# Four of 32 embedding fields fetched by one-hot products on TensorE instead of by gathers, in a DLRM tower on one Trainium2 core

## The chip, the cores and the metric

One Trainium2 chip, one NeuronCore of it. The metric is the device time of one execution in microseconds (us), the median over the runs. Engines: TensorE (PE in the rows; PEld is its weight load), VectorE (DVE), ScalarE (ACT), GpSimd (POOL) and SyncE (SP, which here only issues DMAs).

## What is computed

```python
e = stack([tbl_f[ids[:, f]] for f in range(32)], axis=1)     # 2048 samples x 32 fields x 256
dots = einsum('bnd,bmd->bnm', e, e)                          # 32 x 32 per sample
z = dots[:, iu, ju]                                          # the 496 pairs i < j
h = concatenate([z, dense_ctx], axis=1)                      # 496 + 16
h = maximum(h @ W_top1 + b_top1, 0)                          # 512 x 512
h = maximum(h @ W_top2 + b_top2, 0)                          # 512 x 256
y = h @ W_top3                                               # 256 x 1
```

All is float32. The tables have 1000, 1250 or 12500 rows of 256 numbers; the smallest, of 1000 rows, are nine.

## The kernel before

The work is 2048 samples of 32 fields, that is 65,536 table rows of 1 KB. One indirect DMA of GpSimd (a gather, L121) brings 128 rows: 4 samples ("a quad") with their 32 fields, field by field on 32 partitions. There are 512 gathers. Two of them are a unit; there are 256 units, and 16 row buffers of one unit each (ROWS), so GpSimd may be 16 units ahead of TensorE: before gather pair u it waits for the transposes of unit u-16 (L118).

For each unit TensorE makes four 128x128 transposes (L134, function transposes), ScalarE copies the result from PSUM to SBUF (evacuate, L207), and one unit later TensorE makes 32 small products (gram, L147): for each of 8 samples and two halves of the 256 columns, the 32x32 matrix of dot products. Eight units (16 quads, 64 samples) fill a PSUM bank; then VectorE spreads it with 16 copies (regroup, L240) into `pairs`, where 128 samples are one tile. There are 16 tiles. For a tile TensorE makes layer 1 (64 products, L160), ScalarE its ReLU (relu1, L216), TensorE layer 2 (16 products, L172), VectorE its ReLU (relu2, L251), TensorE layer 3 (L179), VectorE takes the score (L257), and SP stores it.

Each engine works through its list in order, and that list is written by hand: TensorE goes through transposes(u), gram(u-1), and puts layer 1 of the tile before behind the third unit of a tile, layer 2 behind the tenth and layer 3 behind the thirteenth. SP loads the indices first and then the dense features and the weights; w1 is 2 MB in 128 rows of 16 KB.

Of the kernel before, what the change touches and what calls it, by code (L numbers as in the profile page):

```python
# [5 lines left out]
F32 = mybir.dt.float32  # L6
U32 = mybir.dt.uint32
# [3 lines left out]
P = 128  # L11
N_FIELDS = 32
QUAD = P // N_FIELDS


def dlrm_tower(nc, index_t, base_t, dense_t, table, w1_t, b1_t, w2, b2_t, w3_t, out):
# [3 lines left out]
    NQ = index_t.shape[1]  # L20
# [4 lines left out]
    UQ, FQ, TQ = 2, 16, P // QUAD  # L25
    UNITS, TILES = NQ // UQ, NQ // TQ
    UPF, FPT = FQ // UQ, TQ // FQ
    UPT = UPF * FPT
    M1C, M2C = H1 // P, H2 // P
    KC = N_FIELDS // QUAD  # L30
    ROWS, COLS = 16, 6
    EARLY = 16
    assert HALVES == 2 and ND <= N_FIELDS and UNITS % ROWS == 0

    with ExitStack() as ctx:  # L35
# [8 lines left out]

        raw = sb("raw", [P, NQ], U32)
        base = sb("base", [P, 1], U32)
        index = sb("index", [P, NQ], U32)
        rows = [sb(f"rows{r}", [P, UQ, D]) for r in range(ROWS)]
        cols = [sb(f"cols{r}", [P, HALVES, UQ, P]) for r in range(COLS)]
# [3 lines left out]
        score = sb("score", [1, TILES, P])  # L53
# [5 lines left out]
        identity = sb("identity", [P, P])  # L59

        ps_turn = [pb(f"ps_turn{k}", [P, HALVES, UQ, P]) for k in range(2)]
        ps_gram = [pb(f"ps_gram{k}", [P, FQ, N_FIELDS]) for k in range(2)]
        ps_l1 = pb("ps_l1", [P, M1C, P])
        ps_l23 = pb("ps_l23", [P, 512])

# [7 lines left out]
        identity_zeroed, identity_ready = sem("identity_zeroed"), sem("identity_ready")  # L73
        w1_loaded, w_loaded = sem("w1_loaded"), sem("w_loaded")
        l1_done, hidden1_ready = sem("l1_done"), sem("hidden1_ready")
        l2_done, hidden2_ready = sem("l2_done"), sem("hidden2_ready")
        l3_done, score_ready = sem("l3_done"), sem("score_ready")
        stored = sem("stored")
# [3 lines left out]
        @block.sync  # L82
        def _(sp):
            sp.dma_start(base[:, :], base_t).then_inc(index_loaded[0], 16)  # L84
            sp.dma_start(raw[:, 0:EARLY], index_t[:, 0:EARLY]).then_inc(index_loaded[0], 16)
            sp.dma_start(raw[:, EARLY:NQ], index_t[:, EARLY:NQ]).then_inc(index_loaded[1], 16)
# [6 lines left out]
            load_dense(1)  # L93
            sp.dma_start(b1_sb[:, :], b1_t).then_inc(w_loaded, 16)
            sp.dma_start(b2_sb[:, :], b2_t).then_inc(w_loaded, 16)
            sp.dma_start(w3_sb[:, :], w3_t).then_inc(w_loaded, 16)
            sp.dma_start(w1_sb[:, :, :], w1_t).then_inc(w1_loaded, 16)
            sp.dma_start(w2_sb[:, :, :], w2.rearrange("(m p) n -> p m n", p=P)).then_inc(w_loaded, 16)
            for n in range(TILES):
                if n + 2 < TILES:  # L100
                    sp.wait_ge(l1_done, n + 1)
                    load_dense(n + 2)
                sp.wait_ge(score_ready, n + 1)
                sp.dma_start(out[n:n + 1, :], score[:, n, :]).then_inc(stored, 16)
            sp.wait_ge(stored, 16 * TILES)

        @block.gpsimd
        def _(pool):
            pool.memset(identity[:, :], 0.0).then_inc(identity_zeroed, 1)  # L109
            pool.wait_ge(identity_zeroed, 1)  # L110
# [3 lines left out]
            for u in range(UNITS):  # L114
                if UQ * u == EARLY:
                    pool.wait_ge(index_ready, 2)
                if u >= ROWS:
                    pool.wait_ge(transposed, u - ROWS + 1)  # L118
                for k in range(UQ):
                    q = UQ * u + k  # L120
                    pool.indirect_dma_start(  # L121
                        out=rows[u % ROWS][:, k, :], out_offset=None, in_=table,
                        in_offset=bass.IndirectOffsetOnAxis(ap=index[:, q:q + 1], axis=0),
                    ).then_inc(gathered[u % ROWS], 16)

        @block.tensor
        def _(pe):
            def transposes(u):
                pe.wait_ge(gathered[u % ROWS], 16 * UQ * (u // ROWS + 1))
                if u >= 2:  # L130
                    pe.wait_ge(cols_ready, u - 1)
                for h in range(HALVES):
                    for k in range(UQ):
                        last = pe.transpose(ps_turn[u % 2][:, h, k, :],  # L134
                                            rows[u % ROWS][:, k, h * P:(h + 1) * P], identity[:, :])
                last.then_inc(transposed, 1)

            def gram(u):
                f = u // UPF
                pe.wait_ge(cols_ready, u + 1)  # L140
                if u % UPF == 0 and f >= 2:
                    pe.wait_ge(pairs_ready, f - 1)
                for k in range(UQ):
                    for h in range(HALVES):
                        for j in range(QUAD):
                            x = cols[u % COLS][:, h, k, N_FIELDS * j:N_FIELDS * (j + 1)]
                            last = pe.matmul(ps_gram[f % 2][N_FIELDS * j:N_FIELDS * (j + 1), UQ * (u % UPF) + k, :],  # L147
                                             x, x, start=(h == 0), stop=(h == HALVES - 1))
                last.then_inc(gram_done, 1)

            def layer1(n):
                pe.wait_ge(pairs_ready, FPT * (n + 1))
# [31 lines left out]
            for u in range(UNITS):  # L184
                transposes(u)
                if u >= 1:
                    gram(u - 1)
                n, at = u // UPT - 1, u % UPT
                if n >= 0:
                    if at == 2:  # L190
                        layer1(n)
                    if at == UPF + 1:
                        layer2(n)
                    if at == UPF + 4:
                        layer3(n)
            gram(UNITS - 1)
# [5 lines left out]
        def _(act):  # L202
            def evacuate(u):
                act.wait_ge(transposed, u + 1)
                if u >= COLS:
                    act.wait_ge(gram_done, u - COLS + 1)
                act.copy(cols[u % COLS][:, :, :, :], ps_turn[u % 2][:, :, :, :]).then_inc(cols_ready, 1)  # L207
# [11 lines left out]
            for u in range(UNITS):  # L219
                evacuate(u)  # L220
                n, at = u // UPT - 1, u % UPT
                if n >= 0 and at == 3:
                    relu1(n)
# [3 lines left out]
        def _(dve):  # L227
            def make_index(i, q0, q1):
                dve.tensor_tensor(index[:, q0:q1], raw[:, q0:q1], base[:, 0:1].broadcast_to([P, q1 - q0]), ALU.add  # L229
                                  ).then_inc(index_ready, 1)  # L230

            def regroup(f):
                n, u = f // FPT, f % FPT
                dve.wait_ge(gram_done, UPF * (f + 1))
# [20 lines left out]
            def take_score(n):  # L255
                dve.wait_ge(l3_done, n + 1)
                dve.tensor_copy(score[:, n, :], ps_l23[0:1, H2:H2 + P]).then_inc(score_ready, 1)  # L257
# [4 lines left out]
            make_index(0, 0, EARLY)  # L262
            dve.wait_ge(index_loaded[1], 16)
            make_index(1, EARLY, NQ)
            for f in range(UNITS // UPF):
                regroup(f)
                n, at = f // FPT - 1, f % FPT
                if n >= 0 and at == 0:
                    relu2(n)
                    take_score(n)  # L270
# [45 lines left out]
```

## Time and profile before

| What | Value |
|---|---|
| median of 3 runs | 672.66 us (671.53 to 675.78) |
| the profiled execution, whole | 671.6 us |
| its span, first to last instruction | 669.8 us |
| mean granted TensorE clock | 0.781 of full speed |
| TensorE matmul busy | 502.9 us, 75% |
| GpSimd busy | 484.8 us, 72% |
| VectorE, ScalarE busy | 203.6 us (30%), 164.8 us (25%) |

Between the span and the whole execution lie 1.8 us. A busy share says how long an engine had an instruction in work, not whether anything waited for it; the views below say that.

### The profile page before, as it was taken

To read this page: it belongs to the slowest core of one execution; us is meant where nothing else is said; L and a number is where in the kernel's file an instruction comes from. 1 tells how busy PE (TensorE), PEld (TensorE's weight loads), DVE (VectorE), ACT (ScalarE), POOL (GpSimd) and SP (SyncE) were. 2 spreads that over 40 slices of the span, in tenths; PEclk is the share of its full clock that TensorE was granted. 3 is DMA by queue.
4 is the path that set the end of the run, shared out by engine and by line. 5 is a ranking of instruction groups with operands and counts; after the bars stand their busy time and mean duration, and the time that the engine had idled before them with its cause. 6 is when DMAs were issued, how large, how long until landed. Compare 5 with 4: busy or idle time off the path is not lost.

```text
span 669.8 us, 23188 instructions
## 1 busy us (share of the span) xinstructions
PE 502.9 (75%) x10560; PEld 416.9 (62%) x10560; DVE 203.6 (30%) x564; ACT 164.8 (25%) x321; POOL 484.8 (72%) x518
## 2 busy tenths in 40 slices
PE   2668778696886968778696877959679696877847
PEld 1547567485764847567485755848567484755736
DVE  0213433204343132433304343231433313343330
ACT  1222213222142222313222141222313222141310
POOL 6777777777777777777777777777777777777730
PEclk9857859687696877859688695977959597696958
DMA  7333333333333333333333333333333333333310
GB/s 246 109 104 111 107 107 109 106 109 106 106 110 104 111 106 107 109 104 112 105 107 110 104 112 104 108 109 103 111 106 109 108 104 109 106 108 109 105 57 0
DMA packets 26753, 71.65 MB, mean 107 GB/s; under 512 B 9232, under 2 KB 10144, under 8 KB 26528
## 3 DMA queue, kind: packets, MB, share of 16 engines
q0 software_dynamic: 24576, 67.14, 34.4%
q1 hardware_dynamic: 2080, 3.03, 1.3%
q8 instruction: 83, 1.36, 0.8%
q14 instruction: 14, 0.11, 0.1%
HBM read 70.13 MB, written 0.01 MB: 105 GB/s over the span
## 4 chain that ended last, share of the span: by engine, by line
POOL 38%; PE 25%; issue 15%; DMA 11%; DVE 9%; ACT 2%; SPq 0%; ACTq 0%
POOL rows L121 38%; PE ps_l L160 15%; DMA rows<-in_table,index 11%; DVE pairs L240 9%; PE ps_turn L134 6%; PE ps_gram L147 3%; ACT hidden L216 1%; PE ps_l L172 1%; ACT cols L207 1%; DMA raw<-in_index_t 0%; DVE hidden L251 0%; PE ps_l L179 0%; SPq L84 0%; DVE score L257 0%; ACTq L35 0%
## 5 line engine op out<-in xcount | busy, mean ns | idle before, releaser
L121 POOL DMA_INDIRECT rows<-in_table,index x512 | 484.1, 946 | 157.6 <-issue 142.2
L240 DVE COPY pairs<-ps_gram 32x128 f32<-32x128 f32 (+1 forms) x512 | 188.2, 368 | 422.9 <-PE ps_gram L147 416.4
L134 PE MATMUL ps_turn<-identity,rows 128*128 128x128 f32 x1024 | 207.1, 336 | 135.2 <-DMA rows<-in_table,index 134.6
L207 ACT COPY cols<-ps_turn 128x512 f32<-128x512 f32 x256 | 148.8, 590 | 482.5 <-PE ps_turn L134 482.5
L134 PEld LDWEIGHTS ps_turn<-identity,rows 128*128 128x128 f32 x1024 | 135.0, 167 | 158.1 <-DMA rows<-in_table,index 139.8
L160 PE MATMUL ps_l<-pairs,w_sb 128*128 128x128 f32 x1024 | 149.3, 319 | 22.6 <-DVE pairs L240 22.6
L160 PEld LDWEIGHTS ps_l<-pairs,w_sb 128*128 128x128 f32 x1024 | 146.2, 233 | 24.6 <-DVE pairs L240 24.5
L147 PEld LDWEIGHTS ps_gram<-cols 128*32 128x32 f32 x8192 | 104.8, 126 | 62.7 <-issue 55.3
L147 PE MATMUL ps_gram<-cols 128*32 128x32 f32 x8192 | 135.5, 214 | 4.3 <-ACT cols L207 3.6
L172 PE MATMUL ps_l<-hidden,w_sb 128*128 128x128 f32 x256 | 32.8, 281 | 1.2 <-ACT hidden L216 1.2
L172 PEld LDWEIGHTS ps_l<-hidden,w_sb 128*128 128x128 f32 x256 | 29.8, 191 | 2.0 <-ACT hidden L216 1.4
L216 ACT ACTIVATE hidden<-ps_l,b_sb 128x128 f32<-128x128 f32 x64 | 18.3, 376 | 16.6 <-PE ps_l L160 16.6
L251 DVE TENSOR_SCALAR hidden<-ps_l,b_sb 128x128 f32<-128x128 f32 x32 | 9.8, 347 | 13.6 <-PE ps_l L172 13.1
L257 DVE COPY score<-ps_l 1x128 f32<-1x128 f32 x16 | 4.5, 279 | 24.4 <-PE ps_l L179 24.4
L179 PE MATMUL ps_l<-hidden,w_sb 128*1 128x128 f32 x64 | 10.5, 290 | 1.8 <-DVE hidden L251 1.7
L179 PEld LDWEIGHTS ps_l<-hidden,w_sb 128*1 128x1 f32 x64 | 4.7, 88 | 3.4 <-DVE hidden L251 2.3
L229 DVE CUSTOM_DVE_ANT_0 index<-base,raw 128x32 uint16<-128x32 uint16 (+1 forms) x2 | 0.8, 425 | 3.0 <-DMA raw<-in_index_t 3.0
L207 ACT ACT_TABLE_LOAD x1 | 1.3, 1283 | 0.7 <-PEq L280 0.7
L260 DVE MEMSET pairs<- 32x128 f32 x2 | 0.3, 165 | 0.8 <-PEq L280 0.8
L111 POOL TENSOR_SCALAR_AFFINE_SELECT identity<-identity 128x128 f32<-128x128 f32 x1 | 0.3, 282 | 0.2 <-POOL identity L109 0.2
L109 POOL MEMSET identity<- 128x128 f32 x1 | 0.2, 204 | 0.3 <-POOLq L280 0.3
L280 POOL MEMSET const-float32-0.0<- 128x1 f32 x1 | 0.1, 98 | 0.2 <-issue 0.2
(3 smaller groups left out, 0.3 us busy)
## 6 DMA issues: line engine op xcount, KB each, us to landing
rows<-in_table,index POOLq DMA_INDIRECT x512, 2.7
w_sb<-in_w_t SPq DMA_DIRECT2D x1, 2048.0 KB, 8.6
w_sb<-in_W_top SPq DMA_DIRECT2D x1, 512.0 KB, 10.9
pairs<-in_dense_t SPq DMA_DIRECT2D x16, 8.0 KB
scores<-score SPq DMA_DIRECT2D x16, 0.5 KB
raw<-in_index_t SPq DMA_DIRECT2D x1, 248.0 KB, 2.6
base<-in_base_t SPq DMA_DIRECT2D x1, 0.5 KB, 2.0
raw<-in_index_t SPq DMA_DIRECT2D x1, 8.0 KB, 1.8
```

Of the source, the lines that this page charges most:

```text
L121: pool.indirect_dma_start(out=rows[u % ROWS][:, k, :], out_offset=None, in_=table, in_offset=bass.IndirectOffsetOnAxis(ap=index[:, q:q + 1 ...
L134: last = pe.transpose(ps_turn[u % 2][:, h, k, :], rows[u % ROWS][:, k, h * P:(h + 1) * P], identity[:, :])
L147: last = pe.matmul(ps_gram[f % 2][N_FIELDS * j:N_FIELDS * (j + 1), UQ * (u % UPF) + k, :], x, x, start=(h == 0), stop=(h == HALVES - 1))
L160: last = pe.matmul(ps_l1[:, m, :], w1_sb[:, c, m * P:(m + 1) * P], pairs[n % 2][:, c, :], start=(c == 0), stop=(c == KC - 1))
L172: last = pe.matmul(ps_l23[:, m * P:(m + 1) * P], w2_sb[:, c, m * P:(m + 1) * P], hidden1[:, c, :], start=(c == 0), stop=(c == M1C - 1))
L179: last = pe.matmul(ps_l23[0:1, H2:H2 + P], w3_sb[:, m:m + 1], hidden2[:, m, :], start=(m == 0), stop=(m == M2C - 1))
L207: act.copy(cols[u % COLS][:, :, :, :], ps_turn[u % 2][:, :, :, :]).then_inc(cols_ready, 1)
L216: last = act.activation(hidden1[:, m, :], ps_l1[:, m, :], ACT.Relu, bias=b1_sb[:, m:m + 1])
L229: dve.tensor_tensor(index[:, q0:q1], raw[:, q0:q1], base[:, 0:1].broadcast_to([P, q1 - q0]), ALU.add).then_inc(index_ready, 1)
L240: last = dve.tensor_copy(pairs[n % 2][N_FIELDS * q:N_FIELDS * (q + 1), c0:KC, TQ * j + FQ * u:TQ * j + FQ * (u + 1)] .rearrange("p c g -> ...
L251: last = dve.tensor_scalar(hidden2[:, m, :], ps_l23[:, m * P:(m + 1) * P], b2_sb[:, m:m + 1], 0.0, ALU.add, ALU.max)
L257: dve.tensor_copy(score[:, n, :], ps_l23[0:1, H2:H2 + P]).then_inc(score_ready, 1)
```

## The change

The last four of the fields with 1000 rows are no longer gathered. They are "picked": for 256 samples and one field, a matrix of zeros and ones (`one_hot`, 1000 table rows as 125 partitions x 8 by 256 samples) is multiplied on TensorE with the table as stationary operand. The operands have the type float32r; so that nothing of the table's precision is lost, each table is split at the start into `table_hi` (a copy in float32r) and `table_lo` (what is left, made on TensorE as identity x raw minus identity x hi, and copied by VectorE). A pick is 32 products of 256 columns: 2 halves x 8 x (hi, lo). There are 32 picks.

The 28 held fields are gathered in another shape: 4 fields of 32 samples in a gather, 14 gathers in a block of 64 samples, 448 in all. A unit is still two gathers and four transposes, and there are 7 units in a block and 32 blocks. There are 8 row buffers in place of 16, and `cols` holds whole blocks. The products for the dot products (gram) now start only when a whole block is there, in two parts in units 1 and 2 of the block behind it; their number is the same.

The diff, cut to its core:

```diff
+    PICKS = 4; FPU = 4; SPG = P // FPU; BLOCK = 64; GROUP = 256
-    ROWS, COLS = 16, 6
+    ROWS, COLS = 8, 3
 @block.sync
+            sp.dma_start(pick_id[:, :], pick_ids).then_inc(ids_loaded, 16)
+            def load_table(j):
+                sp.dma_start(table_raw[j], pick_tables[j].rearrange("(p c) d -> p c d", c=VC)
+                             ).then_inc(table_loaded[j], 16)
+            for j in range(PICKS):
+                load_table(j)
             ... (dense features, then w1, biases, w3, w2)
 @block.gpsimd
+            for t in range(BLOCKS):
+                for u in range(UNITS):
+                    x = UNITS * t + u
+                    if x >= ROWS:
+                        pool.wait_ge(transposed, x - ROWS + 1)
+                    for k in range(SUBS):
+                        pool.indirect_dma_start(...)
 @block.tensor
+            def split_table(j):
+                pe.wait_ge(hi_ready, j + 1)
+                for i in range(PIECES):                       # 4 pieces of 512 columns
+                    x = PIECES * j + i
+                    if x >= 2:
+                        pe.wait_ge(lo_ready, x - 1)
+                    pe.matmul(ps_low[x % 2], identity[0:VP, 0:VP], raw_v[:, 512 * i:512 * (i + 1)], start=True, stop=False)
+                    pe.matmul(ps_low[x % 2], minus_identity[0:VP, 0:VP], hi_v[:, 512 * i:512 * (i + 1)],
+                              start=False, stop=True).then_inc(low_done, 1)
+            def spread_ids(q):
+                pe.matmul(ps_ids[0:VP, 0:GROUP], identity[0:JOBS, q:q + 1].broadcast_to([JOBS, VP]), pick_id_f[:, :],
+                          start=True, stop=True).then_inc(ids_spread, 1)
+            def pick(q, h):
+                if h == 0:
+                    pe.wait_ge(one_hot_ready, q + 1)
+                    if q + 1 < JOBS:
+                        spread_ids(q + 1)
+                    if q < PICKS:
+                        pe.wait_ge(lo_ready, PIECES * (j + 1))
+                    if q >= 1:
+                        pe.wait_ge(stage_ready, q)
+                for c in range(VC):
+                    pe.matmul(ps_pick[:, h, :], table_hi[:, j, c, h * P:(h + 1) * P], one_hot[q % 2][:, c, :], ...)
+                    last = pe.matmul(ps_pick[:, h, :], table_lo[:, j, c, h * P:(h + 1) * P], one_hot[q % 2][:, c, :], ...)
+            def gram(b, part):
+                if part == 0:
+                    pe.wait_ge(cols_ready, UNITS * (b + 1))
+                    pe.wait_ge(picks_placed, b + 1)
+            for t in range(BLOCKS):
+                for u in range(UNITS):
+                    transposes(UNITS * t + u)
+                    if t == 0 and u >= UNITS - PICKS:
+                        split_table(u - (UNITS - PICKS))
+                    if t == 1 and u < PICKS:
+                        pick(u, 0)
+                        pick(u, 1)
+                    if t == 2 and u == 0:
+                        gram(0, 0)
+                        gram(0, 1)
+                    if t >= 2 and u in (1, 2):
+                        gram(t - 1, u - 1)
+                    if t >= 3 and t % 2 == 1:
+                        if u == 1: layer2((t - 3) // 2)
+                        if u == 3: layer3((t - 3) // 2)
+                    q = PICKS + 2 * ((t - 1) // 2)
+                    if 1 <= t and q < JOBS:
+                        if t % 2 == 1 and u >= 4:
+                            pick(q + (u - 4) // 2, (u - 4) % 2)
+                        if t % 2 == 0 and u == 3:
+                            pick(q + 1, 1)
+                    if t >= 2 and t % 2 == 0 and u == 6:
+                        layer1((t - 2) // 2)
 @block.scalar
+            # take_pick(q): ps_pick -> stage, 128x512; place(b): stage -> cols, 128x512
+                    if t == 0 and u >= UNITS - PICKS:
+                        act.wait_ge(table_loaded[j], 16)
+                        act.copy(table_hi[:, j, :, :], table_raw[j]).then_inc(hi_ready, 1)
+                    evacuate(t, u)
+                    if t >= 2 and u == 0:
+                        place(t - 1)
+                    ... (take_pick behind units 5 and 3, relu1 behind unit 6 of even blocks)
 @block.vector
+            def make_one_hot(q):                              # 8 x (125 x 256), from PSUM
+                dve.wait_ge(ids_spread, q + 1)
+                if q >= 2:
+                    dve.wait_ge(picked, q - 1)
+                for c in range(VC):
+                    last = dve.tensor_scalar(one_hot[q % 2][:, c, :], ps_ids[0:VP, 0:GROUP], row_number[:, c:c + 1],
+                                             1.0, ALU.is_equal, ALU.mult)
+            ... (16 copies of table_lo, then make_one_hot(0) to (3))
+            for t in range(1, BLOCKS + 1):
+                q = PICKS + 2 * ((t - 1) // 2)
+                if t % 2 == 1 and q < JOBS:
+                    make_one_hot(q)
+                if t % 2 == 1 and t >= 3:
+                    relu2((t - 3) // 2)
+                if t == 2:
+                    regroup(0)
+                if t >= 2:
+                    regroup(t - 1)
+                if t % 2 == 1 and t >= 3:
+                    take_score((t - 3) // 2)
+                if t % 2 == 1 and q < JOBS:
+                    make_one_hot(q + 1)
```

Each block t is thus 7 units of TensorE's list; two blocks, an even one and the odd one behind it, make a pair, with one tile's layers, two picks and two regroups.

## Rows read from the trace of the kernel before

**Rows 1.** The page: busy time of three engines, and the granted clock in 40 slices.
```profile
PE 502.9 (75%) x10560; PEld 416.9 (62%) x10560; DVE 203.6 (30%) x564; ACT 164.8 (25%) x321; POOL 484.8 (72%) x518
...
PEclk9857859687696877859688695977959597696958
```

**Rows 2.** The page: shares of the span in the chain that ended last.
```profile
POOL rows L121 38%; PE ps_l L160 15%; DMA rows<-in_table,index 11%; DVE pairs L240 9%; PE ps_turn L134 6%; PE ps_gram L147 3%; ACT hidden L216 1%; PE ps_l L172 1%; ACT cols L207 1%; DMA raw<-in_index_t 0%; DVE hidden L251 0%; PE ps_l L179 0%; SPq L84 0%; DVE score L257 0%; ACTq L35 0%
```

**Rows 3.** Waits: engine, line, for whom; us in total, times, longest.
```profile
POOL rows L121 <- issue: 142.2, 467, 0.3
...
POOL rows L121 <- PE ps_turn L134: 13.4, 44, 0.3
```

**Rows 4.** Busy time of each engine from the first gather to the last.
```profile
3.46:642.29 638.83, 483.19 (x512) 0.78 0.38 112
```

**Rows 5.** Timeline, a stretch at full clock (start, us, engine, line, operation, count).
```profile
305.84 0.66 PE L134 MATMUL ps_turn<-identity,rows 128*128 128x128 f32 x4
...
306.42 0.46 PE L147 MATMUL ps_gram<-cols 128*32 128x32 f32 x32
...
306.81 0.66 PE L134 MATMUL ps_turn<-identity,rows 128*128 128x128 f32 x4
...
312.89 2.05 PE L172 MATMUL ps_l<-hidden,w_sb 128*128 128x128 f32 x16
...
318.23 0.61 DVE L251 TENSOR_SCALAR hidden<-ps_l,b_sb 128x128 f32<-128x128 f32 x2
```

**Rows 6.** Groups of instructions by form: busy us, mean ns of one.
```profile
L207 ACT COPY cols<-ps_turn 128x512 f32<-128x512 f32 x256 | 148.8, 590 | 482.5 <-PE ps_turn L134 482.5
...
L240 DVE COPY pairs<-ps_gram 32x128 f32<-32x128 f32 x384 | 144.2, 375 | 5.2
...
L251 DVE TENSOR_SCALAR hidden<-ps_l,b_sb 128x128 f32<-128x128 f32 x32 | 9.8, 347 | 13.6 <-PE ps_l L172 13.1
```

**Rows 7.** Windows inside the last layer 1: clock 0.5, then 1.0.
```profile
653.70:658.60 4.90, 4.90 (x23) 4.90 (x24) 0.00 (x0) 0.00 (x0) 0.00 (x0) 0.50 0.00 0
658.60:663.40 4.80, 4.80 (x43) 4.63 (x42) 0.00 (x0) 0.00 (x0) 0.00 (x0) 1.00 0.00 0
```

**Rows 8.** The tail's timeline, behind the last gather.
```profile
642.28 0.95 POOL L121 DMA_INDIRECT rows<-in_table,index  x1 [0.30 <-issue]
...
645.14 1.12 PE L134 MATMUL ps_turn<-identity,rows 128*128 128x128 f32 x4 [0.66 <-DMA rows<-in_table,index]
...
646.29 0.59 ACT L207 COPY cols<-ps_turn 128x512 f32<-128x512 f32 x1 [1.77 <-PE ps_turn L134]
...
647.66 5.99 DVE L240 COPY pairs<-ps_gram 32x112 f32<-32x112 f32 x16 [7.72 <-PE ps_gram L147]
...
653.70 9.71 PE L160 MATMUL ps_l<-pairs,w_sb 128*128 128x128 f32 x64 [6.11 <-DVE pairs L240]
663.46 1.14 ACT L216 ACTIVATE hidden<-ps_l,b_sb 128x128 f32<-128x128 f32 x4 [16.58 <-PE ps_l L160]
```

**Rows 9.** The start: first gather, issue of w1, first transposes.
```profile
3.46 1.10 POOL L121 DMA_INDIRECT rows<-in_table,index  x1 [1.99 <-DVE index L229]
...
4.50 0.43 SPq L97 DMA_DIRECT2D w_sb<-in_w_t  x1
...
12.37 1.09 PE L134 MATMUL ps_turn<-identity,rows 128*128 128x128 f32 x4 [12.37 <-DMA rows<-in_table,index]
```

**Rows 10.** DMA issues: KB each, median us from issue to landing.
```profile
rows<-in_table,index POOLq DMA_INDIRECT x512, 2.7
w_sb<-in_w_t SPq DMA_DIRECT2D x1, 2048.0 KB, 8.6
```

**Rows 11.** Window while w1 is on its way (last three: clock, DMA share, GB/s).
```profile
8.00:12.00 4.00, 0.00 (x0) 0.00 (x0) 0.00 (x0) 0.00 (x0) 3.09 (x4) 1.00 0.95 400
```

**Rows 12.** Windows (busy us of PE, PEld, DVE, ACT, POOL; clock; DMA share; GB/s).
```profile
313.80:317.20 3.40, 2.95 (x83) 2.46 (x81) 3.28 (x10) 1.17 (x2) 2.58 (x3) 1.00 0.40 116
317.20:320.60 3.40, 1.64 (x40) 1.02 (x40) 1.85 (x6) 0.59 (x1) 2.70 (x3) 1.00 0.38 107
320.60:324.00 3.40, 3.13 (x68) 2.34 (x72) 0.00 (x0) 0.86 (x2) 2.49 (x4) 0.51 0.34 98
...
40.00:50.00 10.00, 6.81 (x144) 4.96 (x144) 0.55 (x2) 2.34 (x4) 7.57 (x9) 0.50 0.36 107
```

More of the change, by code:

```diff
@@ L6 @@
 F32 = mybir.dt.float32
+F32R = mybir.dt.float32r
+I32 = mybir.dt.int32
 U32 = mybir.dt.uint32
@@ L43, in sem @@
             return ctx.enter_context(nc.semaphore(name))
[L45 to L49, printed above, removed]
+        raw = sb("raw", [P, BLOCKS, GATHERS], U32)
+        base = sb("base", [P, GATHERS], U32)
+        index = sb("index", [P, BLOCKS, GATHERS], U32)
+        rows = [sb(f"rows{r}", [P, SUBS, D]) for r in range(ROWS)]
+        cols = [sb(f"cols{r}", [P, HALVES, BLOCK, N_FIELDS]) for r in range(COLS)]
+        stage = [sb(f"stage{g}", [P, HALVES, GROUP, PICKS]) for g in range(2)]
         pairs = [sb(f"pairs{p}", [P, KC, P]) for p in range(2)]
@@ L183, in _ @@
             pe.wait_ge(identity_ready, 1)
[L184 to L196, printed above, removed]
+            pe.wait_ge(ids_ready, 1)
+            spread_ids(0)
+            pe.wait_ge(minus_ready, 1)
+            for t in range(BLOCKS):
[12 more added lines that the diff above has]
+                    if t >= 3 and t % 2 == 1:
+                        if u == 1:
+                            layer2((t - 3) // 2)
+                        if u == 3:
+                            layer3((t - 3) // 2)
+                    q = PICKS + 2 * ((t - 1) // 2)
[6 more added lines that the diff above has]
+                        layer1((t - 2) // 2)
+            gram(BLOCKS - 1, 0)
+            gram(BLOCKS - 1, 1)
             layer1(TILES - 1)
@@ L289 @@
     n_samples = ids.shape[0]
-    tiles = n_samples // P
-    rows = [inputs[f"tbl_{f}"].shape[0] for f in range(N_FIELDS)]
-    starts = np.array([sum(rows[:f]) for f in range(N_FIELDS)], np.uint32)
-    index_t = dram("index_t", ids.reshape(-1, P).T.astype(np.uint32))
-    base_t = dram("base_t", np.tile(starts, QUAD).reshape(P, 1))
-    table = dram("table", np.concatenate([np.asarray(inputs[f"tbl_{f}"]) for f in range(N_FIELDS)]))
+    tiles, blocks, groups = n_samples // P, n_samples // BLOCK, n_samples // GROUP
+    tables = [np.asarray(inputs[f"tbl_{f}"]) for f in range(N_FIELDS)]
+    smallest = min(t.shape[0] for t in tables)
+    picks = [f for f in range(N_FIELDS) if tables[f].shape[0] == smallest][-PICKS:]
+    held = [f for f in range(N_FIELDS) if f not in picks]
+    order = held + picks
+    units = len(held) // FPU
+    starts = np.cumsum([0] + [tables[f].shape[0] for f in held])[:-1].astype(np.uint32)
+    index_t = ids[:, held].reshape(blocks, BLOCK // SPG, SPG, units, FPU).transpose(2, 4, 0, 3, 1)
+    index_t = dram("index_t", index_t.reshape(P, -1).astype(np.uint32))
+    base_t = dram("base_t", np.repeat(np.tile(starts.reshape(units, FPU).T, (SPG, 1)), BLOCK // SPG, axis=1))
+    table = dram("table", np.concatenate([tables[f] for f in held]))
+    pick_ids = dram("pick_ids", ids[:, picks].reshape(groups, GROUP, PICKS).transpose(0, 2, 1)
+                    .reshape(groups * PICKS, GROUP).astype(np.int32))
+    pick_tables = [dram(f"tbl_{f}", tables[f]) for f in picks]
     dense = np.asarray(inputs["dense_ctx"])
```

212 lines of the change are left out of this document (142 added, 70 removed).

## The prediction

> **What bounds the kernel now.** No engine is full [rows 1]: TensorE is busy 75% of the span, GpSimd 72%. So I go to the chain that ended last: GpSimd's gathers have 38% of the span there, far more than anything else [rows 2]. Then to the waits: 467 gathers were preceded only by "issue", 0.30 us each, and the 44 charged to TensorE's transposes have the same 0.30 us; GpSimd never waits for a buffer [rows 3]. Last the pace: 512 gathers start between 3.46 and 642.28 us, one every 638.82/511 = 1.250 us, of which 0.94 are the instruction [rows 4]. The kernel is a metronome: 3.5 us start, 639 us of gathers, and a tail of 27.5 us behind the last issue. All else waits for rows. The clock shows it: it moves between its two levels, and the mean is 0.78 [rows 1].
>
> **Removed: 64 gathers.** The last gather would start at 3.5 + 447 x 1.250 = 562.3 us. The tail grows: the transposes come 2.9 us behind the last issue and the evacuation ends 1.7 us later [rows 8] as before, but then a placing copy of 0.6 us (a 128x512 copy by ScalarE) [rows 6] and the gram of a whole block, 128 products in place of 32, stand ahead of the regroup. Those 32 take 0.39 us warm [rows 5] and at most twice that cold; with 0.5 the other 96 cost +1.6; tail 27.5 + 0.6 + 1.6 = 29.7 us. If the metronome still rules: 592.0 us of span, 593.8 with the 1.8 us around it. That needs two things: that TensorE's list keeps up with 35.0 us for a pair of blocks (28 gathers), and that the start does not fall behind. I find neither.
>
> **The unit costs.** At full clock transposes and gram of a unit follow each other in 0.97 us: 0.58 to the gram, 0.39 to the next transposes [rows 5]; transposes alone some 0.45, a gram part of 64 products 0.74. Layer 1 runs at 4.80/43 = 0.112 us a product at full clock and 4.90/23 = 0.213 at half [rows 7], so 7.1 us warm, 13.6 cold; layer 2 in a row 1.8 us [rows 5]. A regroup is 6.0 us [rows 8], a 128x512 copy 0.59, relu1 1.15. Not in the trace: a float32r product. Bounds: twice the rate of float32 (256 columns in 0.11 us, as 128 now) or the same rate (0.22). A float32 product of 128 columns takes 0.112 us, 268 cycles of 2.4 GHz, two passes over its columns [rows 7]; float32r keeps less of the number (hence the two table parts), so I take one pass, 0.11. The other end is a rival. Half a pick is 16 x 0.11 = 1.8 us warm. One-hot: two VectorE operations of 128 columns take 0.61, the first 0.35, so they follow at 0.26 [rows 5, 6]; 256 columns lie between 0.39 (fixed part 0.13 kept, columns doubled) and 0.52; eight are 3.1 to 4.2 us, I take 3.3.
>
> **The pair of blocks, as a chain.** From the end of a layer 1 (even block, unit 6), all warm:
> - relu1 1.2, evacuate 0.6, place 0.6 (ScalarE's list), then gram part 0: 3.25
> - layer 2 1.8, transposes and gram part 1 1.3: 6.4
> - regroup 6.05: 12.5; score 0.35, then make_one_hot(q+1) 3.3, which stands behind the regroup in VectorE's list: 16.2. TensorE's other work there (transposes of units 3 to 6, layer 3, spread_ids, pick(q) in two halves) ends at 13, then it stands before pick(q+1)
> - spread_ids 0.2 and half a pick 1.8: 18.2
> - even block: transposes, evacuate, place 1.9, gram 0.75, transposes and gram 1.3: 22.2
> - regroup 6.05: 28.3; TensorE's rest of the pick and its transposes are done at 26 and it waits
> - layer 1 7.2: 35.6.
>
> So 35.6 us warm against 35.0 of the gathers. Nothing of this chain is idle time of gathers: TensorE's list is in order, so while it waits for the one-hot or the regroup, the transposes behind that wait stand too, and with 8 buffers in place of 16 GpSimd stops some 14 us later (8 units of 2.5 us, less 2.5 for the unit itself, 2.9 to landing and the transposes). Before, the longest stop was a layer 1 of 9.7 us [rows 8], and 16 buffers hid it.
>
> **The clock on that chain.** The waits of 3 and 2 us are where it can fall: from 317.2 to 320.6 us TensorE had little to do, 1.64 us busy, and then stood at 1.2 GHz; from 313.8 to 317.2 it was busy 2.95 us and stayed at 2.4 [rows 12]. With gathers alone to wait for it is cold for the whole of 40 to 50 us [rows 12]. Behind a wait layer 1 ran 4.9 us at half clock [rows 7]. A cold half pick costs +1.8; a cold start of layer 1 +2.5. I take the first in every pair, and the second as open: 37.5 us a pair, ends 35.6 and 42.
>
> **The start.** TensorE's list holds split_table(0) to (3) behind units 3 to 6 of block 0, each behind its table's load and a hi copy by ScalarE (2048 columns: at most 4 x 0.59, I take 1.9). The tables are 1 MB each. While w1 was loading the DMAs moved 400 GB/s at a share of 0.95 [rows 11], 26 GB/s for each of 16; gathers take some 0.36 of each [rows 12]. How many of the 16 carry a table? The loads of the trace have 128 rows; the table's copy has 125, which no 16 can share equally; equal shares are possible for 5 at most. Bounds: 16 (1 MB: 3.8 us beside gathers), 1 (60 us). I take 5: 205 KB each at 26 x 0.65 = 17 GB/s, 12 us a table. With the first on its way at 4.4 us they land at 16.4, 28.4, 40.4 and, gathers having stopped, 48. The Trainium skill, page "DMA: Bandwidth & Descriptors", section "Why a DMA increments its semaphore by 16 and not by 1", states that a load issued by SP uses the largest number up to 16 that divides the slowest dimension, 5 for 125. By it the sum is the one below; by an even spread it is that of the second rival; no row here shows a load with such a number of rows.
>
> A split is 4 pieces of 512 columns, a float32 and a float32r product: 0.67 us warm, 1.3 cold, and behind a wait it is cold: 5.2. Split 0 ends at 23.5, 1 at 35.5, 2 at 47.5, 3 at 55.3. Unit 14's gathers, due at 38.5, need the transposes of unit 6, 48.4: 10 us late. Then a one-hot (59.5), pick 0 cold (64.7), three more picks of 3.6 plus 0.45 transposes and 0.45 for its ScalarE copy: 78.2; the three halves behind units 4 to 6 end at 85.1. Block 2 has two grams and two regroups ahead of layer 1: 2 + 12.1; layer 1 starts at 99 and, cold at first, ends at 109. With 16 engines the tables cost no wait, the splits run together, and it ends at 84.
>
> **The sum.** Layer 1 of tile 0 ends at 109; 13 more pairs of 37.5 bring that of tile 13 to 596.5. GpSimd then has 13 units left, 25 x 1.25 = 31.3 us from the next transposes (0.6 us) to the last issue, and the tail 29.7, which is 61.6 us together: 658.1 us of span, 659.9 for the execution. The 671.6 us of the profiled run stand 1.1 under the median, so **661**. Hidden at no cost: ScalarE's 14 evacuations, picks and places (18 x 0.59 in 37 us), make_one_hot(q) under layer 1, the index and id copies of VectorE in the first 6 us, iota on GpSimd ahead of its wait for the index (2.0 us) [rows 9], tables against gathers on 11 of 16 engines.
>
> **Rivals.**
> - The metronome rules (start 23 us late at most, pairs of 35.0): 594 to 618. For it: the warm chain is only 0.6 us over 35.0, and my VectorE figures may be high. Against it: the waits are in order, and the clock. Chance 0.13.
> - The tables load on 16 engines: layer 1 of tile 0 ends 25 us earlier, 636. For it: w1 had 8.6 us for 2 MB [rows 10], every load seen is spread. Chance 0.2.
> - The clock goes against it (the other side): TensorE falls to half clock at both waits, and layer 1, the halved pick and the grams between run cold; pairs of 40 us give 693. It decides from 109 + 13C + 61.6 + 1.8 = 671.6, that is C = 38.4 us a pair. For it: the waits of 3 and 2 us, and the fall at 320.6 us behind less idle time at a stretch. Against it: in a dense layer 1 the clock was back after 4.9 us [rows 7]. Chance 0.2.
> - float32r is no faster than float32: a half pick +1.8 on the chain (13 x 1.8 = 23) and 14 in the start: 698, more when picks of 3.6 us no longer fit under regroup and one-hot. It is also the case in which the change doesn't do what it says. Chance 0.1.
> - The likeliest, the chain at 37 to 38: 0.37, own range 648 to 675.
>
> **How the numbers follow.** About 1% is what a measurement of this kernel can tell from no change, here 666 to 679. Faster: the metronome 0.13, 16 engines 0.17 of its 0.2, the likeliest 0.22 (its range lies mostly under 666): 0.52. Same: 0.12 of the likeliest, 0.03 of 16 engines, 0.02 of the two slow cases: 0.17. Slower: 0.28 of the two slow cases, 0.03 of the likeliest: 0.31. The range reaches into both ends: 612 to 700.
>
> **What would show it.** In the profile after: gathers with waits on TensorE's transposes in place of "issue" only; TensorE waiting for the one-hot (VectorE) at the pick line once a pair, and for pairs at layer 1; table loads with 12 us to landing; gathers idle around 38 to 55 us; layer 1 ends 37.5 us apart. It is wrong if gathers stay at 1.25 us throughout (metronome), if layer 1 ends are 35.0 or over 38.4 apart, if a pick's products follow at 0.22 us at full clock, or if the tables land within 5 us of each other.

## The result, and the profile after

| | before | changed kernel |
|---|---|---|
| median | 672.33 us (4 runs) | 794.38 us (4 runs, 789.0 to 796.5) |
| ratio | | 1.179, 95% interval 1.173 to 1.186 |
| span of the profiled execution | 669.8 us | 791.5 us |
| mean granted clock | 0.781 | 0.905 |
| layer 1 of a tile, end to end | 40.1 us | 45.2 us a pair of blocks |

The change makes the kernel 18% slower. 661 us was predicted, 1.7% faster than before, with a range up to 700 and a chance of 0.31 for slower. The hand-overs that the prediction describes are there, one by one; their sizes are not. Three single executions stood apart from the others of their kernel and are in no ratio below: 705.1 us in e5 (the profiled one), 649.6 us in e11, and 1511.9 us in e6, which nothing here explains.

The page of the changed kernel: busy times, and the chain that ended last.

```profile
PE 609.8 (77%) x11568; PEld 530.7 (67%) x11568; DVE 318.4 (40%) x837; ACT 197.8 (25%) x358; POOL 424.3 (54%) x455
...
PE 52%; DVE 26%; issue 11%; DMA 6%; ACT 4%; SPq 0%; ACTq 0%
DVE pairs L385 19%; PE ps_l L244 17%; PE ps_gram L230 15%; DMA cols<-in_tbl 6%; DVE one_hot L373 6%; PE ps_turn L181 5%; PE ps_pick L213 5%; PE ps_pick L215 4%; PE ps_l L256 4%; ACT hidden L332 2%; ACT cols L310 2%; PE ps_ids L199 2%; ACT stage L315 1%; PE ps_l L193 1%; DVE score L404 0%
```

GpSimd's gathers, 38% of the chain before [rows 2], are gone from it. TensorE has 52% and VectorE 26%, the regroup alone 19%. The waits say the same from the other side (engine, line, for whom; us in total, times, longest):

```profile
POOL rows L168 <- PE ps_turn L181: 205.4, 76, 11.5
...
PE ps_ids L199 <- DVE one_hot L373: 36.6, 13, 3.5
...
PE ps_gram L230 <- issue: 32.2, 30, 2.5
...
PE ps_l L244 <- DVE pairs L385: 26.8, 14, 6.1
```

Before, no such wait was longer than 0.3 us [rows 3]. Now GpSimd stands for 205 us, up to 11.5 at a time. TensorE waits 13 times for a one-hot (once a pair, as forecast), 14 times for a regroup at layer 1, and 30 times for nothing that this view shows ("issue") at a gram product, most often in the middle of gram.

One pair of blocks in the timeline, from the end of a layer 1 at 304.4 us to the end of the next at 349.6. TensorE first (the pick products, 32 single rows each, are left out), then VectorE:

```profile
304.28 1.04 PE L181 MATMUL ps_turn<-identity,rows 128*128 128x128 f32 x8
306.71 1.82 PE L230 MATMUL ps_gram<-cols 128*32 128x32 f32 x128 [1.40 <-ACT cols L310]
308.47 2.05 PE L256 MATMUL ps_l<-hidden,w_sb 128*128 128x128 f32 x16
310.35 0.60 PE L181 MATMUL ps_turn<-identity,rows 128*128 128x128 f32 x4
310.88 2.03 PE L230 MATMUL ps_gram<-cols 128*32 128x32 f32 x128
...
322.94 0.78 PE L199 MATMUL ps_ids<-pick_id_f,identity 32*125 32x256 f32 x2 [2.82 <-DVE one_hot L373]
...
327.07 1.04 PE L181 MATMUL ps_turn<-identity,rows 128*128 128x128 f32 x8
328.91 1.61 PE L230 MATMUL ps_gram<-cols 128*32 128x32 f32 x128 [0.80 <-ACT cols L310]
330.45 0.66 PE L181 MATMUL ps_turn<-identity,rows 128*128 128x128 f32 x4
331.03 1.60 PE L230 MATMUL ps_gram<-cols 128*32 128x32 f32 x100
334.00 0.45 PE L230 MATMUL ps_gram<-cols 128*32 128x32 f32 x28 [1.37 <-issue]
...
340.69 4.57 PE L244 MATMUL ps_l<-pairs,w_sb 128*128 128x128 f32 x25 [1.43 <-DVE pairs L385]
```

```profile
313.26 6.18 DVE L385 COPY pairs<-ps_gram 32x112 f32<-32x112 f32 x16 [2.10 <-PE ps_gram L230]
319.47 0.28 DVE L404 COPY score<-ps_l 1x128 f32<-1x128 f32 x1
319.68 3.21 DVE L373 TENSOR_SCALAR one_hot<-ps_ids,row_number 125x256 fp32r<-125x256 f32 x8
334.50 6.14 DVE L385 COPY pairs<-ps_gram 32x112 f32<-32x112 f32 x16 [11.61 <-PE ps_gram L230]
```

Read it by hand-overs. VectorE starts its regroup when gram part 1 is done (312.9) and its one-hot right behind (319.68 to 322.89); TensorE, whose list has the pick next, does nothing else until 322.94. Then half a pick, gram, a second regroup (334.50 to 340.64) and layer 1 right behind it (340.69). Three windows of the same pair (busy PE, PEld, DVE, ACT, POOL; clock; DMA share; GB/s):

```profile
319.90:322.90 3.00, 0.22 (x3) 0.00 (x0) 2.99 (x8) 1.31 (x2) 2.26 (x3) 1.00 0.31 89
323.60:326.80 3.20, 3.20 (x15) 3.15 (x15) 0.00 (x0) 0.00 (x0) 0.00 (x0) 0.50 0.14 41
...
340.70:344.00 3.30, 3.30 (x16) 3.30 (x17) 3.20 (x8) 0.00 (x0) 2.58 (x3) 0.51 0.41 119
```

TensorE stands idle for 3 us, and the half pick behind it runs at 1.2 GHz; so does the beginning of layer 1. In the second window GpSimd does nothing at all; as the wait list has it, it stands for TensorE's transposes, with its 8 buffers in use.

### The profile page after: what moved, and what is told of

It reads as the page before. It is cut to its first block, busy times and chain, and to the rows that moved or that the text cites. A ratio compares the mean times of both kernels' runs of the same rounds, so it can differ in the third digit from the quotient of the medians.

```text
span 791.5 us, 25288 instructions
## 1 busy us (share of the span) xinstructions
PE 609.8 (77%) x11568; PEld 530.7 (67%) x11568; DVE 318.4 (40%) x837; ACT 197.8 (25%) x358; POOL 424.3 (54%) x455
## 4 chain that ended last, share of the span: by engine, by line
PE 52%; DVE 26%; issue 11%; DMA 6%; ACT 4%; SPq 0%; ACTq 0%
DVE pairs L385 19%; PE ps_l L244 17%; PE ps_gram L230 15%; DMA cols<-in_tbl 6%; DVE one_hot L373 6%; PE ps_turn L181 5%; PE ps_pick L213 5%; PE ps_pick L215 4%; PE ps_l L256 4%; ACT hidden L332 2%; ACT cols L310 2%; PE ps_ids L199 2%; ACT stage L315 1%; PE ps_l L193 1%; DVE score L404 0%
## 5 line engine op out<-in xcount | busy, mean ns | idle before, releaser
L168 POOL DMA_INDIRECT rows<-in_table,index x448 | 423.5, 945 | 320.8 <-PE ps_turn L181 205.4
L181 PE MATMUL ps_turn<-identity,rows 128*128 128x128 f32 x896 | 143.5, 296 | 23.4 <-ACT cols L310 11.6
L230 PE MATMUL ps_gram<-cols 128*32 128x32 f32 x8192 | 112.8, 201 | 63.3 <-issue 32.2
L213 PE MATMUL ps_pick<-one_hot,table_hi 125*128 125x256 f32 x512 | 151.0, 324 | 4.0 <-DVE one_hot L373 2.5
L244 PE MATMUL ps_l<-pairs,w_sb 128*128 128x128 f32 x1024 | 132.3, 296 | 26.9 <-DVE pairs L385 26.8
L215 PE MATMUL ps_pick<-one_hot,table_lo 125*128 125x256 f32 x512 | 144.6, 312 | 0.0
L181 PEld LDWEIGHTS ps_turn<-identity,rows 128*128 128x128 f32 x896 | 109.9, 151 | 36.1 <-issue 27.9
L213 PEld LDWEIGHTS ps_pick<-one_hot,table_hi 125*128 125x128 f32 x512 | 113.0, 221 | 16.8 <-issue 13.1
L215 PEld LDWEIGHTS ps_pick<-one_hot,table_lo 125*128 125x128 f32 x512 | 113.8, 222 | 0.8 <-issue 0.8
L373 DVE TENSOR_SCALAR one_hot<-ps_ids,row_number 125x256 fp32r<-125x256 f32 x256 | 102.9, 471 | 10.8 <-PE ps_ids L199 10.4
L199 PE MATMUL ps_ids<-pick_id_f,identity 32*125 32x256 f32 x64 | 26.6, 500 | 41.9 <-DVE one_hot L373 36.6
L315 ACT COPY stage<-ps_pick 128x512 f32<-128x512 f32 x32 | 34.4, 1074 | 61.2 <-PE ps_pick L215 61.2
```

Source lines behind the costliest of these rows:

```text
L168: pool.indirect_dma_start(out=rows[x % ROWS][:, k, :], out_offset=None, in_=table, in_offset=bass.IndirectOffsetOnAxis(ap=index[:, t, SUBS ...
L181: last = pe.transpose(ps_turn[x % 2][:, h, SPG * k:SPG * (k + 1), :], rows[x % ROWS][:, k, h * P:(h + 1) * P], identity[:, :])
L199: pe.matmul(ps_ids[0:VP, 0:GROUP], identity[0:JOBS, q:q + 1].broadcast_to([JOBS, VP]), pick_id_f[:, :], start=True, stop=True).then_inc(id ...
L213: pe.matmul(ps_pick[:, h, :], table_hi[:, j, c, h * P:(h + 1) * P], one_hot[q % 2][:, c, :], start=(c == 0), stop=False)
L215: last = pe.matmul(ps_pick[:, h, :], table_lo[:, j, c, h * P:(h + 1) * P], one_hot[q % 2][:, c, :], start=False, stop=(c == VC - 1))
L230: last = pe.matmul(ps_gram[b % 2][N_FIELDS * j:N_FIELDS * (j + 1), g, :], x, x, start=(h == 0), stop=(h == HALVES - 1))
```

## The experiments

Each is the changed kernel with one edit, unless said otherwise. "Pair" is the mean distance of 13 ends of layer 1, tiles 0 to 13.

**e1, the second pick two units later.**

```diff
-                        if t % 2 == 1 and u >= 4:
-                            pick(q + (u - 4) // 2, (u - 4) % 2)
-                        if t % 2 == 0 and u == 3:
-                            pick(q + 1, 1)
+                        if t % 2 == 1 and u in (4, 5):
+                            pick(q, u - 4)
+                        if t % 2 == 0 and u in (3, 4):
+                            pick(q + 1, u - 3)
```
(and take_pick(q + 1) on ScalarE at u == 4)

> The second pick of a pair goes two units later (units 3 and 4 of the even block, behind its gram parts), so TensorE has work while VectorE makes the regroup and the one-hot; nothing else changes. In-order chain theory: the 3.0 us wait for the one-hot goes, the 1.4 us wait for the pairs shrinks to under 1, the half pick runs warm (1.5 us less): pairs of layer 1 ends 45.2 us to 39 to 40, time 793 us to 710 to 725. Rival, TensorE is simply full of work: no change (within 1%). Rival, GpSimd's 8 buffers alone set the pace: no change either.

Measured: 707.03 us, 1.0525 of the kernel before (1.0475 to 1.0574); pair 38.4 us. The same amount of work, 87 us less, a little more than forecast: 13 pairs at 6.8 us make 88. The wait for the one-hot fell from 13 times to once, and the mean clock rose from 0.905 to 0.949. Its waits:

```profile
PE ps_gram L230 <- issue: 36.4, 39, 2.7
...
PE ps_l L244 <- DVE pairs L385: 10.7, 4, 6.1
...
PE ps_ids L199 <- DVE one_hot L373: 3.5, 1, 3.5
```

The rivals fall: with a full TensorE, or with 8 buffers that set the pace by themselves, the time would not have moved.

**e2, the tables loaded in pieces that 16 engines can share.**

```diff
+                table_v = pick_tables[j].rearrange("(p c) d -> p c d", c=VC)
+                sp.dma_start(table_raw[j][0:EVEN], table_v[0:EVEN]).then_inc(table_loaded[j], 16)
+                sp.dma_start(table_raw[j][EVEN:VP], table_v[EVEN:VP]).then_inc(table_loaded[j], 16)
```
(EVEN is 112, and ScalarE waits for both)

> Each table is loaded in two pieces, 112 rows (16 equal shares) and 13 rows, in place of one piece of 125. If a load of 125 rows goes over 5 of the 16 DMA engines: the four tables land within some 15 us instead of 54, the first layer 1 ends about 20 to 25 us earlier, the pairs behind it stay at 45 us, and the time falls by 20 to 25 us, to 768 to 773. Rival, the table loads are slow for another reason (8 KB rows, the gathers beside them): no change. Rival, start time is caught up later anyway: the first layer 1 ends earlier and the time does not change.

Measured: 783.48 us (ratio 1.163, 1.161 to 1.165), 11 us less than the changed kernel; first layer 1 ended at 112.1 in place of 124.0, pair 45.4. Half of what was expected. Of the changed kernel ScalarE's timeline shows when each table was there:

```profile
18.65 1.90 ACT L342 CAST table_hi<-stage 125x2048 fp32r<-125x2048 f32 x1
...
30.35 1.90 ACT L342 CAST table_hi<-stage 125x2048 fp32r<-125x2048 f32 x1 [8.90 <-DMA stage<-in_tbl]
...
44.08 1.90 ACT L342 CAST table_hi<-cols 125x2048 fp32r<-125x2048 f32 x1 [11.35 <-DMA cols<-in_tbl]
...
53.75 1.90 ACT L342 CAST table_hi<-cols 125x2048 fp32r<-125x2048 f32 x1 [7.28 <-DMA cols<-in_tbl]
```

The trace's completion events name the cause more directly. Each of these tables ends with 5 of them, beside one at its issue; the tables are there at 15.6, 30.3, 44.1 and 53.7 us. In e2 each ends with 29 (16 for 112 rows, 13 for 13 rows), at 9.7, 15.8, 21.8 and 27.6 us, and no cast waits for a load (the four begin between 24.7 and 40.0 us). So the number of rows sets how many engines carry a load: 5 for 125. But the DMA engines that now carry tables all carry gathers too. TensorE's first transposes in e2:

```profile
15.20 1.09 PE L183 MATMUL ps_turn<-identity,rows 128*128 128x128 f32 x4 [8.61 <-DMA rows<-in_table,index]
...
26.51 1.12 PE L183 MATMUL ps_turn<-identity,rows 128*128 128x128 f32 x4 [2.30 <-DMA rows<-in_table,index]
```

Unit 3 is turned at 26.5 us, in the changed kernel at 19.7. What the tables gained, the gathers half gave back. What is won at the start stays won to the end (12 us there, 11 in the time).

**e3, half of the gram products left out** (the second 128 of each row's 256 numbers).

> Leaves out half of the gram products (the second 128 of the 256 numbers of a row), nothing else. My sum counted 64 rows of the trace for a gram part where there are 128, 1.7 us in place of 0.74. If these terms stand on the chain in full: four parts a pair, each 0.8 us less, and the 1.4 us pause for code inside a part goes too: pairs 45.2 to 40.5 to 42, time to 725 to 745. If gram is hidden under other waits: within 1% of 793.

Measured: 699.49 us, one execution, where 725 to 745 was expected; pair 39.1, 6.1 us less, more than the 3.2 to 4.7 expected. "Issue" in gram fell from 32.2 us to this:

```profile
PE ps_gram L229 <- issue: 10.3, 11, 2.2
```

So gram stands on the chain in full: the stretches of a pair that hold it are 5.3 us shorter (the table behind e9). Half of its instructions takes two thirds of the pauses with it.

**e4, the kernel before with 8 row buffers** (ROWS = 8 in place of 16).

> The kernel before with 8 row buffers in place of 16, nothing else. If only the chain of the new kernel makes the smaller buffer felt: the longest stop of TensorE is a layer 1 of 10 us and some, under the 14 us that 8 buffers cover, so the time stays within 1% of 672 us. Rival, 8 buffers are themselves the loss: over 700 us.

Measured: 673.25 us, ratio 0.9999 (0.9990 to 1.0009). In the kernel before, 8 buffers cost nothing. Whether 16 would have helped the changed kernel was not run; no gather stands on its chain.

**e5, e1 and the picks placed ahead of the evacuation** (`place(t - 1)` before `evacuate(t, u)` in unit 0).

> The first edit (second pick two units later) and one more: ScalarE places a block's picks ahead of the next block's first evacuation, not behind it. On the chain theory the gram part 0 of each block starts 0.5 us earlier, two blocks a pair: 38.4 us a pair to 37.2 to 37.6, time 707 us to 690 to 697. Rival, TensorE is by now full: 704 to 708.

Measured: 696.26 us, ratio 1.0341 (1.0316 to 1.0367): in the forecast's range, some 11 us less than e1. Its pairs are 38.6 in the profiled execution of 705 us and can't be compared, so where the gain arises is not shown.

**e6, e5 with gram in four parts.** (`range(FQ // 4 * part, FQ // 4 * (part + 1))`, parts in units 0 to 3.)

> The kernel of e5 with the gram of a block in four parts (units 0 to 3) in place of two (units 1 and 2), so that its instructions stand less densely. Theory, the pauses inside gram (36 us in e1's profile, 2.3 us a pair, each some 1.5 us behind the start of a 16 KB load of code) come from using up instructions faster than they are loaded: most of them go, and pairs fall by 1 to 2 us below e5, though the regroup starts one unit later. Rival, the pauses come with the amount of code, whatever its density: they stay, and pairs are as long as in e5 or 1 us longer.

Measured: 690.24 us, ratio 1.0258 (1.0234 to 1.0282); pair 37.5.

```profile
PE ps_gram L230 <- issue: 44.9, 35, 2.5
```

A gain of some 5 us, but not for the reason given: the pauses did not go. My theory of dense instructions falls in this form. What sets a pause's length is in the traces: of the 21 pauses over 0.3 us between two gram products of the changed kernel, each begins 0.1 to 1.8 us behind the start of a 16 KB code load and ends 1.2 to 1.6 us behind that load's end. For the 249 such pauses of all fourteen traces the second figure is 1.1 to 1.6 us without exception. That fits a TensorE that has used up its code and waits for the next piece; no run changes the loads alone. The kernel before has 83 such loads and the changed one 91, but before only one pause in gram, of 0.6 us: there gram came in small pieces between waits for gathers.

**e7, table_lo on VectorE.** The 32 products and 16 copies of split_table are out; the one-hot of pick 0 is made first.

```diff
+                dve.tensor_tensor(table_lo[:, j, :, :], table_raw[j], table_hi[:, j, :, :], ALU.subtract
+                                  ).then_inc(lo_ready, 1)
```

> The changed kernel with table_lo made by VectorE (raw minus hi, 4 subtractions of 125x2048) in place of 32 products on TensorE and 16 copies. The splits take TensorE 5.8 us each in block 0, two of the four under waits for tables. Chain theory: the first layer 1 ends 8 to 12 us earlier (about 113), pairs stay at 45, time 793 us to 781 to 785. Rival, only the landing of the tables counts: within 3 us of 793.

Measured: 781.98 us, one execution. The time is as expected, its parts are not: the first layer 1 ended at 117.3, 7 us earlier in place of 8 to 12, the pairs took 45.4, and the stretch behind the layer 1 of tile 13 was 7.5 us shorter (72.4 us), which nothing in the edit explains. That the time was hit is in part luck.

**e8, picks of 4 products in place of 32** (7 of 8 table parts left out).

> Leaves out 7 of the 8 table parts in every pick: 4 products in place of 32. 28 fewer at 0.117 us, two picks a pair, is 6.6 us of TensorE work a pair at full clock. On the chain only the half pick behind the one-hot counts (14 products, 1.6 us, 2.9 at half clock) and the longer wait before it gives the rest back: pairs 45.2 to 42 to 43.5, the start 3 x 3.3 us shorter at most (VectorE's one-hot of 3.2 us sets the pace there): time 793 to 745 to 765. Rival, TensorE full: pairs fall by the whole 6.6 us and more, time under 705.

Measured: 783.38 us, one execution; pair 45.0, the first layer 1 ended 8 us earlier (116.4). Neither theory: seven eighths of all picks gone, and the pair is as long as in the changed kernel. The waits of e8:

```profile
PE ps_ids L199 <- DVE one_hot L373: 78.0, 18, 6.0
...
PE ps_l L244 <- DVE pairs L385: 49.4, 16, 6.1
```

And its span with its mean clock:

```profile
core 0: 781.6 us, clock 0.810
```

The wait for the one-hot doubled (36.6 to 78.0 us), that for the pairs nearly (26.8 to 49.4), and the clock went from 0.905 to 0.810. The Trainium skill, page "TensorE: Matmul & The Clock Gate", Part 1, has the low clock as the default state that activity lifts; e8 agrees, with 0.810 for less work against 0.905. The part of the picks that is off the chain is hidden under VectorE's work. The part on it was gained and lost again, as the table behind e9 shows: from the end of the one-hot to the even block's gram the pair is 2.5 us shorter, but from there to the regroup it is 1.1 us longer and at layer 1 1.5 us. All 13 of these layers 1 took 8.8 us or more in e8, as only 6 of 13 did in the changed kernel, where the others took 7.3 to 7.4. One of them, and the clock at its beginning:

```profile
334.77 9.55 PE L244 MATMUL ps_l<-pairs,w_sb 128*128 128x128 f32 x64 [3.08 <-DVE pairs L385]
...
334.80:337.80 3.00, 3.00 (x14) 3.00 (x15) 3.00 (x8) 0.00 (x0) 2.39 (x3) 0.50 0.36 104
```

So at layer 1 it is the lower clock that took the gain back. Of the 1.1 us ahead of the regroup, clock and code pauses (38.3 us a run in place of 32.2) are not separated.

**e9, e8 and one one-hot operation in place of eight.**

> The kernel of e8 (4 products of a pick in place of 32) and one of the 8 one-hot operations in place of 8: the rest of both is left out. In e8 the pairs stayed at 45 us, the wait for the one-hot took what the picks left. Chain theory: the 7 operations of 0.40 us behind the regroup come off the pair in full, and the 7 for the other pick, under layer 1, come off nowhere: pairs 45 to 42 us, time 783 to 740 to 752. Rival, the regroup and the clock set the pair: 44 to 45 us stay, 775 to 785.

Measured: 734.39 us, one execution; pair 42.2 as expected, the time under the 740 to 752 expected. From e8, which has the same picks, 49 us: 2.8 us a pair, which is 7 x 0.40, and 12 us at the start. Only the one-hot that TensorE waits for counts, but that one in full.

The pair by its hand-overs, means of 13 pairs in us, from the timelines:

| Stretch | changed kernel | e3 | e8 | e9 |
|---|---|---|---|---|
| end of layer 1 to the odd block's regroup (gram in it) | 9.1 | 6.6 | 9.2 | 9.6 |
| regroup, score and one-hot | 9.6 | 9.6 | 9.5 | 6.8 |
| end of the one-hot to the even block's gram (half pick in it) | 6.5 | 5.6 | 4.0 | 3.7 |
| even block's gram to its regroup | 5.5 | 2.7 | 6.6 | 6.8 |
| regroup to the start of layer 1 | 6.3 | 6.2 | 6.1 | 6.1 |
| layer 1 | 8.2 | 8.4 | 9.7 | 9.2 |
| pair | 45.2 | 39.1 | 45.0 | 42.2 |

**e10, all edits together** (e1, e2, e5, e6, e7).

> Second pick later, picks placed first, gram in quarters, tables on 16 engines, table_lo on VectorE. The gains of the single edits at the start (10 and 11 us) add up only in part, as the gathers of the start have to share the DMA engines with the tables: first layer 1 ends at 98 to 105, pairs stay at 37.5, time 690 to 668 to 678. Rival, the start is caught up: 688 to 692.

Measured: 656.36 us, ratio 0.9757 (0.9743 to 0.9771), better than the 668 to 678 forecast; pair 37.8, the first layer 1 ended at 92.5. The two edits at the start add up to more than their sum of 19 us: 29 us against e6's 121.6. That neither edit hides the other any more is my reading; no run separates it.

**e11, e10 with layer 1 one unit later.**

```diff
+                        if u == 0:
+                            layer1((t - 3) // 2)
                         if u == 1:
                             layer2((t - 3) // 2)
...
-                    if t >= 2 and t % 2 == 0 and u == 6:
-                        layer1((t - 2) // 2)
```
(relu1 on ScalarE moves along)

> The kernel of e10 with layer 1 (and its ReLU on ScalarE) one unit later, in unit 0 of the odd block behind gram part 0, so that the regroup is covered by one unit more and gram part 0 does not wait behind the ReLU. Chain theory: the waits for pairs (17 us in e6's profile) and for ScalarE at gram (19 us) mostly go, pairs fall by 1.5 to 2.5 us to about 35.5, near the gathers' 35.0, and the time to 645 to 655, under the kernel before. Rival, TensorE is full by now: no gain over e10.

Measured: 639.94 us, ratio **0.9525** (0.9500 to 0.9549): 5% faster than the kernel before, with the same picks, gathers and buffers as the changed kernel. Pair 36.3. Its waits:

```profile
POOL rows L170 <- PE ps_turn L183: 44.0, 39, 3.6
...
PE ps_gram L219 <- issue: 22.2, 32, 2.2
...
PE ps_gram L219 <- ACT cols L297: 18.7, 15, 1.3
...
PE ps_l L233 <- DVE pairs L372: 8.1, 2, 6.1
```

The waits for pairs went from 15.5 us in e10 to 8.1, of which one is the tail; those for ScalarE at gram did not go, against what was expected. The time is under the 645 to 655 forecast, and the pair 0.8 us over. What TensorE stands for "issue" at gram fell from 44.8 to 22.2 us though the amount of code is the same, so it is not the amount alone that counts.

**e12, e11 with thin picks.**

> The kernel of e11 with 4 products of a pick in place of 32 (7 of 8 table parts left out). In the changed kernel this edit moved no pair (e8). If in e11 TensorE itself is the bound, with 36.3 us a pair against the gathers' 35.0: pairs fall to 35.0 to 35.5 and no further, since the gathers take over, and the start is some 8 us shorter: 640 us to 612 to 625. Rival, waits and the lower clock give it back again as in e8: 636 us or more.

Measured: 610.09 us, one execution; pairs 35.0 from tile 2 on, the gathers' pace. The two before took 31.8 and 31.5. The waits show who took over:

```profile
POOL rows L170 <- issue: 121.9, 400, 0.3
PEld ps_turn L183 <- DMA rows<-in_table,index: 76.9, 52, 4.4
...
PE ps_turn L183 <- DMA rows<-in_table,index: 71.2, 48, 8.8
```

TensorE waits for rows again. The same edit that moved no pair in e8 takes 1.3 us off each from tile 2 on here, where the gathers stop it: in e11 TensorE's own work sets the pace, in the changed kernel its waits do.

## Why the prediction was wrong

By its own steps:

- **Bound before, and 64 gathers less**: right. The gathers kept 1.25 us where nothing stopped them, and with the picks thinned and the waits gone (e12) the metronome came back at 35.0 us a pair.
- **The chain of a pair**: right in its order, and every hand-over of it is in the timeline above. The sum was 35.6 us warm, 37.5 with the half pick cold, and 45.2 was measured. The step that failed is the unit cost of a **gram part**, "a gram part of 64 products 0.74". A part is 64 calls in the code, but a float32 product is two rows of the trace: the 16 calls for a unit in the code before (8 samples, two halves) are the 32 rows of [rows 5]. The description of the kernel before counts such rows as products, the prediction then took calls for rows. A part has 128 rows. Measured in the pair above: part 0 and, with its transposes, part 1 take 1.8 and 2.5 us in the odd block, 1.5 and (without the pause) 2.6 in the even one; I had 0.75, 1.3, 0.75 and 1.3, that is 4.3 us a pair too little. The row that I used was right, my count of it was half.
- **Pauses inside gram**: not foreseen, 1.4 us in the pair shown. Of the kernel before the same view has one, of 0.6 us:

```profile
PE ps_gram L147 <- issue: 0.6, 1, 0.6
```

- **spread_ids**: 0.7 us in place of 0.2, the same miscount of a float32 product.
- **The clock**: the cold half pick was right, +1.6 us for 1.8 forecast; the cold start of layer 1, left open, cost 1.7 in the pair shown (8.9 us in place of 7.2) and came at 6 of the first 14 layers 1. Together 35.6 + 4.3 + 1.4 + 0.5 + 1.6 + 1.7 = 45.1 for the 45.2 of that pair.
- **One-hot**: 3.2 us for 3.3 forecast, a regroup 6.2 for 6.05, a product of a pick 0.117 us behind the one before it for 0.11: right, and with it the float32r rival fell. The figure for the pick came out by luck in part. The prediction took one pass for it and two for a float32 product, read from a row of 0.112 us; but that row is half a product. A float32 call of 128 columns costs 0.224 us, a float32r one of 256 columns 0.117, so the rate is about four times, not twice.
- **The start**: loads on 5 engines: right, and by e2 caused by the 125 rows, as the Trainium skill's page "DMA: Bandwidth & Descriptors", section "Why a DMA increments its semaphore by 16 and not by 1", has it; the 5 and 29 completion events agree. The tables were there at 15.6, 30.3, 44.1 and 53.7 us, where 16.4, 28.4, 40.4 and 48 were forecast. The first layer 1 ended at 124.0, forecast 109: the last table 5.7 us late, a piece of a split 1.09 us where I had 0.67 (the count of float32 rows again), two grams at half their size, and one-hots 5.3 us apart where I had 4.5.
- **The end**: behind the layer 1 of tile 13 came 79.9 us, forecast 61.6. I let GpSimd's gathers end it; but the pairs of tiles 14 and 15 took 36.4 and 37.0 us, and the last gather was out at 744.7, 46.8 us ahead of the end in place of 29.7. These two pairs have no pick and no one-hot any more. So they also show what picks and one-hots cost a pair in this order of the list, some 8.8 us of 45.2, and that without them the list in blocks would still be slower than the gathers' 35.0.

The difference to the sum is 13 x 7.7 = 100 us in the pairs, 15 at the start, 18 at the end: 133, from 658 of span to 791.

The slow rival named the clock as its reason and 38.4 us a pair as the point of decision. Its reason was the smaller part of what came, and its point held only with the start and the end as I had summed them: e1 has 38.4 us a pair and took 707. The wide range still missed, since both its ends rested on the same wrong count.

## What to carry to other kernels

Count what an engine does in rows of the trace, not in calls of the code, before a duration of the trace is multiplied with it. In an in-order list a wait costs everything behind it: put between a product and its consumer on another engine as much other work as that engine needs (e1 and e11 changed no work and gave 87 and 16 us). An engine's work off the chain is worth nothing when removed, and what is saved on the chain can be lost to a lower clock behind the longer wait (e8), until the waits are gone and it is the bound (e12); so order the list first, and then count its load.

## What was not expected of the hardware

- A load of 125 rows takes 5 of the 16 DMA engines (5 completion events): 1 MB tables come 10 to 15 us apart beside gathers; loaded as 112 rows and 13 they have 29 events and come 6 us apart.
- TensorE pauses of up to 2.5 us at gram in the changed kernel, 32.2 us in all ("issue"). In all traces here the pauses over 0.3 us between gram products end 1.1 to 1.6 us behind the end of a 16 KB load of code. Less code makes them fewer (10.3 us in e3), gram in smaller pieces does not (44.9 us in e6), and a shift of layer 1 halves them (44.8 to 22.2 us, e10 to e11).
- ScalarE's copy of a pick from PSUM (128x512, written in single numbers 16 bytes apart) takes 1.07 us, the evacuation of the same size, written in runs of 16 bytes, 0.60.
- Seven eighths of the products of the picks left out changed the pairs by nothing (45.2 to 45.0 us), with the clock down from 0.905 to 0.810.
